# Launch phase of a fused attention and feed-forward kernel: transposes of a constant on TensorE, bias products on column tiles, two chunks turned by TensorE, weight parts in other places

## The reference

```python
x = x + attn(layernorm(x))        # attn normalises once more, with ln_g and ln_b
x = x + ffn(layernorm(x))
# attn
qkv  = x_norm @ W_qkv + b_qkv     # x_norm = norm(x) * ln_g + ln_b
gate = sigmoid(x @ W_gate + b_gate); gate = gate / (mean(gate) + eps)
q = relu(q * gate) ** 2 + eps;  k = relu(k * gate) ** 2 + eps
# 16 heads of 32; kv and k are summed over all earlier rows
num = q . sum(k v^T);  den = q . sum(k) + eps;  out = (num / den) @ W_proj + b_proj
# ffn
out = gelu((x @ U1) @ V1 + b1) @ U2 @ V2 + b2
```

## Time and profile before

| what | us |
|---|---|
| median of 3 runs | 1725.85 |
| lowest and highest of them | 1725.49, 1728.28 |
| the profiled execution, its own time | 1725.1 |
| its span | 1723.4 |

### The profile page before, as it was taken

One profiled execution on the slowest core, in us unless ns is written; L12 is line 12 of the kernel. 1 busy time (PEld: TensorE's weight loads), 2 busy tenths in 40 slices (PEclk: granted clock), 3 DMA queues, 4 the chain that ended last, 5 costly groups with the idle time before them and its releaser, 6 DMA issues.

```text
span 1723.4 us, 39521 instructions
## 1 busy us (share of the span) xinstructions
PE 1696.4 (98%) x16477; PEld 1431.6 (83%) x16477; DVE 1393.9 (81%) x2159; ACT 666.2 (39%) x1242; POOL 885.5 (51%) x1026
## 2 busy tenths in 40 slices
PE   7999999999999999999999999999999999999997
PEld 4788888888888888888888888888888888888886
DVE  6888888888887887887888888888888878878875
ACT  5243343343333333434433433433343334344332
POOL 4365555554555555555555555545555555555540
PEclk9999999999999999999999999999999999999999
DMA  7211111011111111110111110110111111101100
GB/s 222 59 36 53 36 51 50 24 54 53 34 53 41 34 53 50 37 53 26 49 53 35 52 49 26 53 53 33 53 41 34 53 49 38 53 27 47 41 20 26
DMA packets 61938, 82.09 MB, mean 48 GB/s; under 512 B 14953, under 2 KB 25601, under 8 KB 61761
## 3 DMA queue, kind: packets, MB, share of 16 engines
q1 hardware_dynamic: 60896, 77.99, 14.4%
q10 hardware_dynamic: 864, 1.57, 0.3%
HBM read 62.60 MB, written 16.94 MB: 46 GB/s over the span
## 4 chain that ended last, share of the span: by engine, by line
PE 94%; DVE 4%; issue 1%; ACT 1%; DMA 0%; POOL 0%; SPq 0%; DVEq 0%; POOLq 0%
PE ps_a L828 11%; PE ps_a L829 10%; PE ps_a L830 10%; PE scores L828 7%; PE scores L830 7%; PE scores L829 7%; PE ps_h L828 4%; PE ps_h L829 4%; PE ps_h L830 4%; PE scores L958 4%; PE scores L994 4%; PE ps_q L828 3%; PE ps_q L829 3%; PE ps_q L830 3%; PE scores L835 3%; PE ps_a L835 2%
## 5 line engine op out<-in xcount | busy, mean ns | idle before, releaser
L432 POOL TENSOR_TENSOR h_lo<-h_full,h_hi 128x512 fp32r<-128x512 f32 x244 | 317.1, 1304 | 255.5 <-DVE h_hi L655 254.6
L828 PE MATMUL ps_a<-wx_hi,zt_hi 128*128 128x512 f32 x768 | 315.4, 411 | 4.6 <-DVE key_sums L768 2.4
L830 PE MATMUL ps_a<-wx_hi,zt_lo 128*128 128x512 f32 x768 | 304.8, 397 | 0.0
L829 PE MATMUL ps_a<-wx_lo,zt_hi 128*128 128x512 f32 x768 | 304.7, 397 | 0.0
L515 ACT ACTIVATE h_full<-ps_h,cols 128x256 f32<-128x256 f32 x512 | 211.0, 475 | 143.7 <-PE ps_h L830 136.6
L655 DVE CAST h_hi<-h_full 128x512 fp32r<-128x512 f32 x256 | 135.4, 538 | 60.1 <-ACT h_full L515 56.5
L828 PEld LDWEIGHTS ps_a<-wx_hi,zt_hi 128*128 128x128 f32 x768 | 145.2, 189 | 42.1 <-DVE zt_lo L610 5.3
L830 PEld LDWEIGHTS ps_a<-wx_hi,zt_lo 128*128 128x128 f32 x768 | 144.8, 189 | 35.5
L526 ACT ACTIVATE query_t<-scores 128x512 f32<-128x512 f32 x64 | 38.4, 599 | 343.3 <-PE scores L835 343.3
L829 PEld LDWEIGHTS ps_a<-wx_lo,zt_hi 128*128 128x128 f32 x768 | 145.1, 189 | 28.6 <-issue 0.5
L386 POOL TENSOR_TENSOR small<-moments,eps_col 128x1 f32<-128x1 f32 x64 | 12.3, 192 | 282.7 <-DVE moments L803 282.7
(11 more groups left out here) (158 smaller groups left out, 4237.0 us busy)
## 6 DMA issues: line engine op xcount, KB each, us to landing
xs<-L_attn_x SPq DMA_DIRECT2D x64, 256.0 KB, 4.1
out<-x1s SPq DMA_DIRECT2D x64, 256.0 KB, 2.1
xt<-x_turned SPq DMA_DIRECT2D x63, 256.0 KB, 4.2
key_sums<-carry_rows SPq DMA_DIRECT2D x60, 256.0 KB, 3.7
rows<-turned_rows SPq DMA_DIRECT2D x63, 64.0 KB, 4.8
x1s<-L_attn_W_gate SPq DMA_DIRECT2D x4, 256.0 KB, 4.0
x1s<-L_ffn_U SPq DMA_DIRECT2D x4, 256.0 KB, 6.8
carry_rows<-key_sums SPq DMA_DIRECT2D x64, 2.0 KB
```

The source lines that it names most:

```text
L432: E.tensor_tensor(h_lo[:, i % SLOTS, :], h_full[:, i % SLOTS, :], h_hi[:, i % SLOTS, :].bitcast(F32), ALU.subtract).then_inc(s["h_lo_ready ...
L828: E.matmul(ps, wh, mh, start=start and i == 0, stop=False)
L829: E.matmul(ps, wh, ml, start=False, stop=False)
L830: mm = E.matmul(ps, wl, mh, start=False, stop=stop and i == last)
```

## The change

- TensorE does 6 transposes of the identity into an unused bank before the vectors are there, 11 after them, and 24 after it has turned chunk 0 (`keep_busy`).
- The bias products use 32 columns of weights in place of 128, and the four calls of a group write to four different column tiles. The four partial sums stand in four groups of 32 partitions; ScalarE copies the bank to SBUF (`bias_part`, into `key_sums`), and TensorE sums and spreads them by one fp32 product with a constant of ones in rows 0, 32, 64 and 96 (`pick`, `bias_sum`). The sums stand after KEY, QUERY and VALUE. The five memsets of `pick` are the first work of VectorE.
- Chunk 1 is treated as chunk 0: VectorE centres it, TensorE turns it between KEY and bias_products(1). Its load of 256 KB from `x_turned`, its trip of means and its `center` are gone.
- W_proj's rows are put in order on the host, by copying alone, so its tiles are one DMA each.
- Staging has two more places, and tiles 16 to 23 are loaded right after the first 16. Tiles 24 to 29 are loaded at the end of step 1.
- Tails: 8 to 11 after the copy of the gate in step 0, 12 to 15 after the keys, 16 and 17 at the end of step 0, 18 and 19 after the copy of the gate in step 1, 20 and 21 after its `z_tail`, 22 and 23 after the copy of the gate in step 2, 24 to 26 after its `z_tail`, 27 at its end, 28 and 29 after the copy of the gate in step 3. Heads 12 to 15 come after the sigmoid of step 0, 16 to 19 after the heads of its keys, 20 to 23 at the end of step 1, 24 to 29 at the end of step 2.
- In step 0 VectorE does `z_tail` of chunk 1 ahead of the statistics of chunk 2, and GpSimd does `add_bias(0)` after the keys.

```diff
@@ staging
-        lnb_wide = probs[:, 0, :].rearrange("p (k n) -> p k n", k=KT)
+        lnb_wide = probs[:, 0, 0:KT * HEAD].rearrange("p (k n) -> p k n", k=KT)
+        stages += [h_full[:, i, :] for i in range(2, 4)]
+        places = list(range(FIRST)) + [0, 1, 2, 3] + 2 * [FIRST, FIRST + 1, 4, 5] + [2, 3]
@@ block.sync
             load_x(Chunk(0, 2))
-            means_out(Chunk(0, 1))
-            load_tiles(range(FIRST, FIRST + 6))
-            means_in(Chunk(0, 1))
+            load_tiles(range(FIRST, SECOND))
@@ block.scalar
-            tile_heads(range(2 * KT, FIRST))
+            tile_heads(range(2 * KT, 3 * KT))
+            def bias_part(i):
+                act.wait_ge(s["stage_bias"], KT * (i + 1))
+                if i:
+                    act.wait_ge(s["bias_sum"], i)
+                E.activation(key_sums[:, :], bias_banks[i][:, :], ACT.Copy).then_inc(s["part_ready"], 1)
+            bias_part(0)
@@ block.vector
             z_tail(Chunk(0, 0))
-            tile_tails(range(KT, 10))
+            tile_tails(range(KT, 2 * KT))
             first_stats(1)
-            tile_tails(range(10, FIRST))
+            dve.wait_ge(s["x_stats"], 4)
+            dve.wait_ge(s["tz_done"], 1)
+            E.tensor_scalar(zs[:, :], xs[:, 1, :], small[:, 1, 2:3], None, ALU.subtract).then_inc(s["z_ready"], 1)
             def add_rows(i):
-                dve.wait_ge(s["stage_bias"], KT * (i + 1))
+                dve.wait_ge(s["bias_sum"], i + 1)
@@ block.tensor
+            def keep_busy(count):
+                for _ in range(count):
+                    E.transpose(ps_h[1][:, 0:P], ident[:, :], ident[:, :])
+            pe.wait_ge(s["consts_pool"], 7)
+            keep_busy(6)
             pe.wait_ge(s["vectors"], 48)
-            pe.wait_ge(s["consts_pool"], 7)
...
-                    E.matmul(bias_banks[i][:, :], lnb_wide[:, k, :], stage(t), start=k == 0, stop=k == KT - 1)\
-                        .then_inc(s["stage_bias"], 1)
+                    E.matmul(bias_banks[i][HEAD * k:HEAD * (k + 1), :], lnb_wide[:, k, :], stage(t), start=True,
+                             stop=True, tile_position=(0, HEAD * k)).then_inc(s["stage_bias"], 1)
+            def bias_sum(i):
+                pe.wait_ge(s["pick_ready"], 5)
+                pe.wait_ge(s["part_ready"], i + 1)
+                E.matmul(bias_banks[i][:, :], pick[:, :], key_sums[:, :], start=True, stop=True)\
+                    .then_inc(s["bias_sum"], 1)
+            keep_busy(11)
             pe.wait_ge(s["z_ready"], 1)
             transpose4(zs, s["tz_done"])
+            keep_busy(24)
@@ step 0 of block.tensor
                     project(KEY, ps_b, s["key_done"])
                     if not c.exists:
+                        bias_sum(0)
+                    if not c.exists:
+                        pe.wait_ge(s["zt_ready"], 1)
+                        pe.wait_ge(s["z_ready"], 2)
+                        transpose4(zs, s["tz_done"])
                         bias_products(1)
                         pe.wait_ge(s["stage_lo"], 3 * KT)
```

More of the change, by code:

```diff
@@ L58, in __init__ @@
         self.first = m is not None and m < BATCHES
+        self.own_turn = m is not None and m < 2
         self.row = (p + off // 4) * P
@@ L313, in load_tiles @@
                     src, slot = tiles[t][0], stage(t)
-                    if t >= FIRST:
-                        before = t % RING if t < FIRST + RING else t - RING
+                    held = [u for u in range(t) if stage_of(u) == stage_of(t)]
+                    if held:
+                        before = held[-1]
                         sp.wait_ge(s["stage_lo"], before + 1)
@@ L360, in step @@
                 load_x(Chunk(p, b + 3))
+                if 4 * p + b == 1:
+                    load_tiles(range(SECOND, len(tiles)))
             steps(step)
@@ L406, in center @@
             def center(c):
-                if not c.exists:
+                if not c.exists or c.own_turn:
                     return
+                before = Chunk(c.p, c.off - 1)
+                if before.own_turn:
+                    pool.wait_ge(s["z_ready"], before.done())
                 mine = xt[:, c.half, :, :]
@@ L531, in step @@
                         .then_inc(s["gate_sig"], 1)
-                if isinstance(p, int) and 4 * p + b == 0:
-                    tile_heads(early_tiles)
+                if 4 * p + b == 0:
+                    tile_heads(range(3 * KT, FIRST))
+                    bias_part(1)
                 if d.exists:
@@ L566, in step @@
                         E.activation(qt_hi[:, :], ps_q[:, 0:GROUP], ACT.Copy).then_inc(s["qt_hi_ready"], 1)
-                if isinstance(p, int) and 4 * p + b < 3:
-                    tile_heads(late_tiles[b])
+                if 4 * p + b == 1:
+                    tile_heads(range(FIRST + 4, SECOND))
+                if 4 * p + b == 2:
+                    tile_heads(range(SECOND, len(tiles)))
             steps(step)
@@ L697, in step @@
                     x1t_tail()
+                if 4 * p + b == 0:
+                    tile_tails(range(3 * KT, FIRST))
                 if b % 2:
@@ L931, in step @@
                     project(QUERY, ps_a, s["query_done"])
+                    if not c.exists:
+                        bias_sum(1)
                 if b % 2 and ffn.exists:
@@ L967, in step @@
                     project(VALUE, ps_a, s["value_done"])
+                    if not c.exists:
+                        bias_sum(2)
                 if ffn.exists and b % 2:
```

85 lines of the change are left out of this document (51 added, 34 removed).

## The result

The kernel after takes 1730.4 us (median; 1726.93 to 1732.05), the kernel before, on the same chip, 1726.56 (1725.18 to 1728.28). The ratio is 1.0021 [1.0014, 1.0027]: 0.2% slower, where 3.55 us of gain were predicted. The loss by the medians, 3.84 us, is also more than rival C, the slowest one, allowed (1728.2, or 2.35 us of loss). The profiled execution has a span of 1726.5 us against 1723.4, so the difference in span, 3.1 us, can be looked for in the trace.

What follows compares the result with a forecast made beforehand. PE, busy 98%, bounds the kernel; in the launch VectorE's chain becomes the new bound. Gain at the first feed-forward product: 4.55 - 0.2 + 0.65 - 1.45 = 3.55 us, so 1725.85 - 3.55 = 1722.3; range 1720.4 to 1726.5.

Steps and rivals of the forecast that it cites:

- rival C: VALUE, and GATE and KEY of step 1: clock falls in PE's new gaps and stays low, 5.9 us lost, 1728.2; chance 0.07.
- Its frame: Start of the first feed-forward product, 91.88 us before: its shift is the whole effect, predicted near 88.3.
- Clock and GATE: Launch, chunk 0: identity transposes raise the clock, so GATE runs 10.6 to 13.4 us, against 15.6.
- Rival A: Launch: transposes leave the clock at 1.2 GHz, GATE runs at 0.43; 1725.0 to 1726.4; chance 0.22.
- Bias products, 1.0 us: Launch: each bias group on four column tiles takes 1.0 us instead of 3.43; bounds 0.86 and 2.1.
- Rival B: Launch bias products: column tiles don't overlap well, 2.1 us a group, gain 1.95, 1723.9; chance 0.08.
- add_rows(0) 19.4: Launch on DVE: after bias_sum(0) at 18.1 and gate_scale at 18.7, add_rows(0) ends at 19.4 us.
- tails 12 to 15 24.4: Launch on DVE: after the key steps at 21.7, tails 12 to 15 take 2.7 us and end at 24.4.
- 25.8 to 28.6: Step 0: VALUE starts after the first query step, when ps_a is free, and runs 25.8 to 28.6 us.
- The serial piece and what follows: Behind VALUE: bias_sum(2) 0.86, add_rows(2) 0.70, values 0.75, to 31.0; key_sums 34.4, GATE of step 1 35.1.
- Step 1, gain 0.65 less 0.2 for the clock: Step 1: fewer tails before the gate copy and a shorter probs wait gain 0.65; a longer low-clock stretch costs 0.2.
- Steps 2 and 3, loss 1.45: Steps 2 and 3: later tails lose 0.25 at once and delay x1t_lo by 1.65, about 1.45 passed to PE.

Runs made afterwards that it cites:

- x1: Kernel after without the 41 transposes of the identity; ratio to the kernel before 1.0028.
- x9: Kernel after with further identity transposes in step 0's gaps and before GATE of step 1, the 30 before VALUE placed ahead of the wait for tails; ratio to before 1.0006.
- x3: Kernel after, but GpSimd's passes over step 0's keys wait until tails 12 to 15 are made; ratio to before 1.0014.
- x8: Kernel after with third bias sum and copy before VALUE, KEY bias row early, GpSimd held in steps 0 and 1, statistics before z_tail, tails spread; ratio to before 0.9962.
- x11: Kernel after, but GpSimd's low half of chunk 3's keys waits until VectorE has its queries; ratio to before 1.0016.
- x4: Kernel after with tails 16 to 20 ahead of add_rows(2) and 21 to 23 behind the values, so fewer in steps 1 to 3; ratio to before 1.0023.
- x13: Kernel after, but GpSimd's output bias addition in step 3 waits until VectorE has the last tail; ratio to before 1.0011.
- x6: Kernel after with the KEY bias row loaded by itself, ahead of the others, with its own semaphore; ratio to before 1.0018.
- x7: Kernel after with identity transposes added in step 0's gaps and before GATE of step 1, the 30 before VALUE behind the wait for tails; ratio to before 1.0027.
- x16: Kernel before with identity transposes: 30 ahead of GATE, 8 ahead of turned keys, 5 ahead of sums, 24 ahead of GATE of step 1; ratio to before 1.0005.
- x5: Kernel after with bias products as before the change: no column tiles, ScalarE copies or partial sums; ratio to before 1.0011.

## Why the prediction was wrong

Its frame held: first product late by 3.08, span longer by 3.1. Its terms, in their order:

- **Clock and GATE: right.** The 24 took 3.35 us (starts 0.13 us apart on average), GATE 10.54 to 13.4, against 10.6 to 13.4. Rival A is out. By the Trainium skill, "TensorE: Matmul & The Clock Gate", Part 4 (PE-mode transpose), it should have come true. For these transposes x1 and x9 show the opposite: without them GATE's first starts are 0.43 us apart, with them 0.23. The trace prints them as fp32 MATMULs and does not show whether they ran in the mode that the page means.
- **Bias products, 1.0 us: right**, and `bias_sum` too (1.02 for 0.86). Rival B is out. The sigmoid ended at 17.5 and gate_scale began at 17.62, a little better than 18.3 and 18.7.
- **"add_rows(0) 19.4": wrong.** It ended at 20.3, as the bias row had not landed. The step asked what stands ahead on each engine, not what the row's transfer waits for. +0.9 us.
- **"tails 12 to 15 24.4": wrong.** The term of 2.7 us measured 4.46. It was priced by rows of tails that ran without GpSimd, and then moved to where GpSimd works on the keys. x3 gives 2.65 back. +1.8 us, so VALUE starts at 28.57 and not at 25.8.
- **"25.8 to 28.6": wrong**, the clock. The sum took 2.8 us for VALUE; it took 4.41, and x9 shows 2.9 for the same products without the gap. +1.6 us. This is rival C's place and mechanism, with a fall after 25.8 and not before it, and with 1.6 us in VALUE of the 2.4 that C had; GATE of step 1 was no worse than before (4.26 against 4.18). C was given 0.07, since the gap was counted as 1.4 us. It was 3.87, because the two errors above had lengthened it; x8, with waits of no more than 0.9 us ahead of VALUE, kept it at 0.23.
- **The serial piece and what follows: right.** From VALUE's end to GATE of step 1 were 6.7 us, 6.5 predicted. So GATE of step 1 is late by 0.9 + 1.8 + 1.6 and 0.3 in small pieces = 4.6 us (39.68 against 35.1), and the launch gains nothing.
- **Step 1, gain 0.65 less 0.2 for the clock: wrong in sign.** From GATE of step 1 to that of step 2 it takes 21.77 us, 21.41 before: 0.36 lost, 0.8 off. The gate was copied early, as foreseen, but with it the queries came to stand beside GpSimd's key_lo (1.66 for 0.69). x11 gives 0.66 back.
- **Steps 2 and 3, loss 1.45: too small.** Step 2 lost 0.87 (0.25 predicted). Its mechanism, the tails, was right and its size was off: in x4, with fewer tails there, step 2 takes 1.2 us less. Step 3 lost 1.86 (11.68 against 9.82; 1.2 predicted), and the excess is the same collision; x13 gives 0.93 back.

Together 4.6 + 0.8 + 0.6 + 0.7 = 6.7 us, against 6.65 between the predicted span (1723.4 - 3.55 = 1719.85) and 1726.5. The steps that failed are thus four: the wait for the bias row, the length of tails 12 to 15 and of other VectorE instructions beside GpSimd, the clock in VALUE, and the cost of the tails in step 2. The wait for the bias row could not be taken out by a run (x6). The Trainium skill, "SBUF — State Buffer" (Who interferes with whom), says that a VectorE instruction with both inputs in SBUF contends with a GpSimd instruction that reads SBUF, and one with at most one SBUF input, outside VectorE's two-port modes, doesn't. The traces agree: L644, L641 and L673 stretch; L666, which reads a bank of PSUM and one SBUF buffer, stays at 0.75 us at 27.67, beside L421 (26.45 to 28.17).

## What to carry to other kernels

When a change moves an instruction of VectorE with two SBUF inputs, price it beside what GpSimd does at the new time; and if it must collide, hold the one that nobody waits for. When a change takes work away from TensorE ahead of a wait, count the gap that it leaves, lengthened by every other error of the sum, and price what follows at the low clock; transposes of a constant in the gap, ahead of every wait in the program's order, kept the clock up at no cost here (x9), while behind the wait they cost more than they gave (x7, x16). A launch that is bound by VectorE does not get faster by a faster TensorE: here 4.4 us less of matmuls gave nothing: with them back (x5) GATE of step 1 started 1.8 us earlier, and the ratio was no worse.
